# Fetching whole groups of table rows on SyncE: eight rows a step instead of seven, for six groups instead of five

## What is computed

```python
h = relu(layernorm(x))
p1 = tanh(h @ pp_W1 + pp_b1) @ pp_W2 + pp_b2
inter = concat([p1[src], p1[dst]]) @ pi_W1 + pi_b1
inter = (inter @ pi_W2 + pi_b2) @ pi_W3          # (edges, 64 * 8)
i1 = einsum('ecb,eb->ec', inter.reshape(-1, 64, 8), edge_attr)
i1 = tanh(i1 @ ii_W1 + ii_b1) @ ii_W2 + ii_b2
out = x + segment_sum(i1, dst, 6250)
```

## Time and profile before

| | us |
|---|---|
| median of 3 runs | 1965.04 (1964.56 to 1967.29) |
| profiled execution, its own time | 1972.48 |
| its span, first to last instruction | 1970.7 |
| PE busy in the span | 1717.0 (87%) |
| DVE | 1453.4 (74%) |
| ACT | 1109.4 (56%) |
| POOL | 1474.1 (75%) |

### The profile page before, as it was taken

One profiled execution on the slowest core, in us unless ns is written; L12 is line 12 of the kernel. 1 busy time (PEld: TensorE's weight loads), 2 busy tenths in 40 slices (PEclk: granted clock), 3 DMA queues, 4 the chain that ended last, 5 costly groups with the idle time before them and its releaser, 6 DMA issues.

```text
span 1970.7 us, 61801 instructions
## 1 busy us (share of the span) xinstructions
PE 1717.0 (87%) x20012; PEld 1125.7 (57%) x20012; DVE 1453.4 (74%) x1937; ACT 1109.4 (56%) x2419; POOL 1474.1 (75%) x1561
## 2 busy tenths in 40 slices
PE   7699999998888888888888888888888988888998
PEld 6366666665555555555555555555555555555666
DVE  7688778787777777777776777777767767777776
ACT  5666666565555555555555555555555655555554
POOL 7777777777777777777777777777777777777774
PEclk8799999999999999999999999999999999999999
DMA  6543333333333333333323333333333333333332
GB/s 139 123 80 64 67 65 60 65 71 65 58 61 60 58 62 58 66 63 57 62 56 61 62 61 66 62 55 61 57 63 64 60 63 62 57 58 55 57 76 47
DMA packets 271300, 128.56 MB, mean 65 GB/s; under 512 B 192747, under 2 KB 243546, under 8 KB 270959
## 3 DMA queue, kind: packets, MB, share of 16 engines
q0 software_dynamic: 49408, 50.69, 16.5%
q10 hardware_dynamic: 55738, 50.10, 10.6%
q1 hardware_dynamic: 165938, 25.50, 7.9%
HBM read 119.48 MB, written 6.00 MB: 64 GB/s over the span
## 4 chain that ended last, share of the span: by engine, by line
POOL 55%; issue 21%; PE 11%; SPq 9%; DMA 1%; ACT 1%; DVE 0%; ACTq 0%; POOLq 0%; DVEq 0%
POOL u_rows L573 55%; SPq L443 6%; PE bank L1388 4%; SPq L440 2%; PE bank L1371 1%; PE bank L1483 1%; SPq L482 1%; PE bank L1395 1%; PE spread_ps L1380 1%; PE bank L1355 1%; DMA p<-L_gnn_pi_W 0%; DMA v_win<-v_tab 0%; PE spread_ps L1217 0%; DMA u_rows<-u_tab,src_e 0%; PE bank L1223 0%
## 5 line engine op out<-in xcount | busy, mean ns | idle before, releaser
L573 POOL DMA_INDIRECT u_rows<-u_tab,src_e x1416 | 1348.0, 952 | 432.0 <-issue 430.7
L996 DVE TENSOR_TENSOR o_sb<-st_sb,spread_ps 128x2048 f32<-128x2048 f32 x391 | 893.6, 2286 | 403.0 <-PE spread_ps L1380 370.3
L761 ACT ACTIVATE st_sb<-bank,s_bias 64x256 f32<-64x256 f32 x1564 | 734.2, 469 | 452.9 <-PE bank L1371 431.3
L1388 PE MATMUL bank<-o_sb,g_sb 128*64 128x256 f32 x6256 | 792.4, 397 | 1.0 <-DVE o_sb L996 0.8
L1388 PEld LDWEIGHTS bank<-o_sb,g_sb 128*64 128x64 f32 x6256 | 427.3, 140 | 225.2 <-issue 23.9
L1371 PE MATMUL bank<-ident,u_rows 128*128 128x128 f32 x1436 | 257.5, 302 | 196.7 <-DMA u_rows<-u_tab,src_e 195.9
L1060 DVE TENSOR_TENSOR hot_t<-loc_bc,bank 126x512 bf16<-126x512 bf16 x391 | 268.6, 687 | 90.6 <-PE bank L1483 44.8
L1371 PEld LDWEIGHTS bank<-ident,u_rows 128*128 128x128 f32 x1436 | 188.7, 191 | 247.5 <-DMA u_rows<-u_tab,src_e 237.8
L1483 PEld LDWEIGHTS bank<-hot,t_sb 128*65 128x65 f32 x3128 | 215.0, 139 | 148.9 <-issue 146.9
L749 ACT ACTIVATE tt_sb<-bank,z_bias 128x256 f32<-128x256 f32 x391 | 185.5, 474 | 157.1 <-PE bank L1388 157.1
L752 ACT COPY t_sb<-bank 128x256 f32<-128x256 f32 x391 | 146.6, 375 | 213.6 <-PE bank L1395 205.1
(11 more groups left out here) (147 smaller groups left out, 350.7 us busy)
## 6 DMA issues: line engine op xcount, KB each, us to landing
loc_bc<-loc_tab ACTq DMA_DIRECT2D x387, 126.0 KB
sp_stage<-u_tab SPq DMA_DIRECT2D x2560, 0.2 KB
u_rows<-u_tab,src_e POOLq DMA_INDIRECT x1416
v_win<-v_tab SPq DMA_DIRECT2D x391, 15.8 KB
basis<-edge_attr SPq DMA_DIRECT2D x24, 256.0 KB
v_tab<-acc_all SPq DMA_DIRECT2D x6, 336.0 KB
basis<-u_tab,src_e POOLq DMA_INDIRECT x100, 2.9
u_tab<-basis SPq DMA_DIRECT2D x6, 224.0 KB
```

Source lines behind the costliest of these rows:

```text
L573: pool.indirect_dma_start(out=u_rows[:, g % UR, j, :] if g >= AHEAD else first_u[:, g - XG, j, :], out_offset=None, in_=u_tab[:, :], in_of ...
L761: last = nc.scalar.activation(tiles[h * D:(h + 1) * D, j], s_ps[part].rearrange("p (q a e) -> p q a e", q=2, a=TILES), ACT.Identity, bias= ...
L996: return nc.vector.tensor_tensor(o_sb[:, r, :, :].rearrange("p c (j e) -> p j c e", j=TILES), st_sb[:, r, :].rearrange("p (j e) -> p j e", ...
L1388: last = nc.tensor.matmul(z_ps[h * D:(h + 1) * D, 0:2 * P], g_sb[:, c, :], o_sb[:, r, c, 2 * h * P:(2 * h + 2) * P], start=(c == 0), stop= ...
```

## The change

Three constants and the semaphores of the first groups change. SP brings the groups 69, 133, 197, 261, 325 and 389 instead of 83, 157, 231, 305 and 380. It begins each 68 steps before its number, at steps 1, 65, 129, 193, 257 and 321, and needs 64 steps of eight rows. Register loads at L440 take sixteen row numbers instead of eight, so there is one in every other step. The groups 7 to 31 had a semaphore each for POOL's gathers; now two neighbours share one, and TensorE waits for both before it uses the first.

```diff
-    ROWS = 7
-    BY_SP = [(83, 4), (157, 78), (231, 152), (305, 226), (380, 300)]
-    AT_ONCE = 8
+    ROWS = 8
+    BY_SP = [(64 * k + 69, 64 * k + 1) for k in range(6)]
+    AT_ONCE = 16
...
-        first_u_in = sems("first_u_in", AHEAD - XG)
+        first_u_in = sems("first_u_in", (AHEAD - XG + 1) // 2)
...
-                        ).then_inc(u_in[g % UR] if g >= AHEAD else first_u_in[g - XG], 16)
+                        ).then_inc(u_in[g % UR] if g >= AHEAD else first_u_in[(g - XG) // 2], 16)
...
-                        pe.wait_ge(first_u_in[g - XG], 64)
+                        pe.wait_ge(first_u_in[(g - XG) // 2], 64 * min(2, AHEAD - XG - (g - XG) // 2 * 2))
```

## The result

| | before | after |
|---|---|---|
| median, us | 1965.72 (1964.56 to 1967.29, 5 runs) | 1975.99 (1975.16 to 1980.59, 5 runs) |
| profiled execution, its span | 1970.7 | 1978.8 |
| POOL's gathers into `u_rows` | 1416 | 1412 |
| TENSOR_LOAD at L440 | 320, median 783 ns | 192, median 1232 ns |
| POOL held by PE | none beyond the gaps it always has | 14.1 us |

The ratio is 1.0056 with a 95% interval of 1.0044 to 1.0068, so 8.6 to 13.4 us more; the forecast was about 8. Both profiled executions are longer than the medians: that of before took 1972.48 us, 7 more (it isn't among the five), and that of after 1980.59, the longest of its five and 4.6 more. So single times near their ends carry some us of their own.

What follows compares the result with a forecast made beforehand. The prediction took POOL's gathers, 5.03 us a group, to bound the kernel. A 9.8 us hold less 2.2 us gained at the end made +7.6, so 1973 us from a median of 1965.04, range 1964 to 2004.

Steps and rivals of the forecast that it cites:

- What bounds the kernel: POOL's gathers, never held, set the pace from 42.5 us to the end: 1.257 us a gather, 5.03 a group.
- The load of sixteen: SP's register load of sixteen row numbers at L440: taken as 1.20 us, 1.26 with the 0.06 around it.
- SP's step: SP's mean step with eight rows and loads of sixteen: 4.81 us instead of 4.51, between 4.60 and 5.00.
- The start: SP's first windows: window 8 leaves at 98.0, 6.6 us later, and window 33 at 221.5, 13.5 us later.
- The hold: POOL's gathers for group 42 wait for group 34's slot until 230.1: 9.8 us lost, not growing afterwards.
- The end: POOL binds PE to about group 386, which PE can start earlier: 2.2 us gained.
- At nothing: Parts taken to cost nothing: shared semaphores of the first groups, the final move at L451, 512 more row transfers.
- The sum: The whole change: 9.8 - 2.2 = +7.6 us on the profiled execution's 1972.5; predicted 1973 from the median shown, 1965.04.
- A load no dearer than eight's: Rival on SP's register loads: sixteen numbers cost about what eight do, the hold shrinks to 3.1, 1966 us; chance 0.21.
- No hold: Rival at POOL's early slots: PE's early groups don't slip behind them, only the end's gain remains, 1963 us; chance 0.05.
- A dear load: Rival on SP's register loads, up to where SP becomes the bound: 1978 us with 1.33, 2001 with 1.45; chance 0.22.
- SP as the bound throughout: Rival on SP's step: from 4.95 us on, POOL is held again and again; 2024 us at 5.00; chance 0.12.

Runs made afterwards that it cites:

- e3: The kernel before with register loads of sixteen row numbers instead of eight and nothing else; ratio 1.0000 to the kernel before.
- e6: The changed kernel with register loads of eight row numbers instead of sixteen, so one in every step; ratio 1.0213 to the kernel before.
- e5: The changed kernel once more, unchanged, on another chip; ratio 1.0043 to the kernel before, median 1978.04 us.
- e1: The changed kernel with SP's reload of x moved from step 8 to step 200; ratio 1.0051 to the kernel before, median 1979.42 us.
- e4: The changed kernel without group 69, the first of SP's six groups, which POOL gathers itself; ratio 1.0025 to the kernel before.
- e7: The changed kernel with other row counts: 8 in steps 1 to 3, 7 to step 33, then 8, and 9 every tenth; ratio 1.0011 to the kernel before.
- e8: The changed kernel with 23 single tiles on SP instead of whole groups, 7 rows in steps 4 to 59, x reloaded at step 200; ratio 0.9988 to before.
- e11: The single-tile version of e8 once more, on another chip; ratio 0.9975 to the kernel before, 1960.62 against 1966.32 us.
- e2: The kernel before with eight rows a step and loads of sixteen, but its own five groups and first steps; ratio 1.0026 to the kernel before.
- e9: The kernel before with loads of sixteen, plus 44 more single-row transfers on SP in step 20; ratio 1.0030 to the kernel before.
- e10: The kernel before with loads of sixteen, plus 44 more single-row transfers on SP in step 200; ratio 0.9999 to the kernel before.

## Why the prediction was right, point by point

**What bounds the kernel.** Right: POOL's total sets the time, and SP's share of the chain before 440 us is no price by itself (e3).

**The load of sixteen.** 1.232 us (taken: 1.20), so 1.29 with what stands around it. The two readings in the earlier trace rows gave 1.14 and 1.33, and the middle was good. By the 200 ns a register of the Trainium skill (Runtime: NRT & Kernel Launch, Instruction fetch mechanics) eight further ones would have made it 2.4; the trace of after doesn't agree, it has (1.232 - 0.783) / 8 = 0.056 us for each.

**SP's step.** 4.78 us, taken 4.81. With loads of eight it is 4.95, taken 5.0 in e6, so the way in which I added the parts is 0.03 to 0.05 too high a step. For e6, which lies just at POOL's rate, that was half the effect; for the changed kernel it hardly counts. The prediction's tightest later place was right too: group 74, some 2 us to spare; measured 3.7, and 2.6 at group 77.

**The start.** Window 8 left at 99.8 and, in e5, 98.2 (taken: 98.0). Between windows 1 and 2 there are 71.99 - 65.71 = 6.3 us instead of 5.1, and most of that excess is the issue of window 1 itself, 1.10 us instead of 0.32; the rest is 0.45 us before the first load of row numbers, which waits for `sp_idx`. The same code had window 8 at 94.8 in e1, so the 98.0 was within what one execution differs from another by. Window 33: 222.8 and 220.4, taken 221.5.

**The hold.** Right in kind and place, 9.8 taken, 14.1 and 11.7 measured. I moved only groups 33 and 34, but group 32's matmuls too, at 204.45 before, came 14.4 us later, and the first wait is for its slot, at group 40. That moves the place, not the sum. The size was missed by three things: groups 32 to 34 slipped by 14.4 to 14.9 us, not 13.5; POOL came there 2.1 us sooner (its first gather into `u_rows` at 167.6 against 169.7); and groups 44 and 45 added 0.8, where the hold was to end at 42.

**The end.** This is the term that was mis-sized: 2.2 us of gain taken, about 0.2 measured. I let PE use group 386 a median 2.9 after its last gather's start. In the changed kernel that is 1941.73 - 1936.80 = 4.9, as before (5.1); in e5 it is 5.0. What happened stands four groups earlier. SP begins to store a part of the output at 1916.67, the DMA engines are 95% busy from 1917 to 1919, and group 382, whose last gather began at 1916.83, can be used only 5.0 us later. PE, idle for 2.99 us, then has half its clock (0.50, the 1.2 GHz level) from 1921 to 1925; the step takes 6.9 us, and at its own 4.1 to 4.5 a step after that PE isn't back at POOL's pace by 386. The lines are SP's store, group 382 on PE, and two stretches (PE, weight load, DVE, ACT, POOL busy; granted clock; DMA share; GB/s):

```profile
1916.67 0.80 SPq L456 DMA_DIRECT2D out<-x_sb  x2
...
1921.85 1.23 PE L1371 MATMUL bank<-ident,u_rows 128*128 128x128 f32 x4 [2.99 <-DMA u_rows<-u_tab,src_e]
...
1917.00:1919.00 2.00, 1.86 (x26) 1.47 (x22) 1.35 (x2) 0.81 (x3) 1.70 (x2) 1.00 0.95 261
...
1921.00:1925.00 4.00, 3.15 (x28) 2.16 (x30) 1.23 (x1) 1.85 (x4) 3.09 (x4) 0.50 0.20 47
```

The kernel before has the same store, at 1912.86, with the DMA engines 92% busy from 1915 to 1917. There the skip at 380 had put POOL ahead, and PE waited for nothing and kept the full clock. So a place that was free while PE was behind POOL's rows cost time once PE waited for them, like the start. That the store made the gather late is read from the two standing side by side; no run moved the store. In e5 waits of 0.90 and 1.23 us at groups 382 and 383 follow the store, and one of 1.19 at 386. e4 agrees by the time: one skip fewer up to group 388 costs 5.2 us, where a whole group is 5.03.

**At nothing.** The shared semaphores, the last move and the 512 further transfers: PE's waits show no entry for the first groups. The shared semaphores weren't tried alone, but e7, e8 and e11 have them, and e8 and e11 are faster than the kernel before, so they cost nothing that can be seen.

**The sum.** From one profile to the other it closes: the hold is 14.1, POOL's first gather begins 0.8 sooner (41.7 against 42.5), the gathers take 5.1 less, and the end gives 0.2. That makes 8.0, and the spans differ by 8.1; the medians differ by 10.3. The 5.1 wasn't in the prediction: with the gaps and without holds a gather takes 1.2545 us in the changed kernel (1896.8 us for 1512; 1.2543 in e5) and 1.2579 in the kernel before (1906.9 for 1516). It isn't shown to come from the change. Over all profiles it is 1.2548 to 1.2582 with five groups on SP (before, e2, e3, e4, e9, e10) and 1.2543 to 1.2563 with six groups or 23 tiles (after, e1, e5, e6, e7, e8, e11): the ranges overlap, and the profiled execution of before, one of the longest of its kernel, has nearly the longest gathers of all. The prediction added its +7.6 to that execution and then set it on the median. So the forecast of 8 came near the 8.6 to 13.4 partly by luck: the hold was too small by 2 to 4, the end's gain too large by 2, and gathers that differ between executions weren't seen.

**The rivals.** A load no dearer than eight's: fell, 1.232. No hold: fell. A dear load, or SP as the bound throughout: fell, but only by 0.17 us a step (4.78 against 4.95): in e6 the same kernel at 4.95 loses another 33 us. e1, whose hold was shorter and whose median wasn't, speaks against none of this: in its profiled execution the hold is 5.3 less than in the changed kernel's, the first gather 0.7 sooner and the gathers 2.7 longer in all, 3.3 less together, and the span is 4.0 shorter. What stays open is what makes the start of SP and POOL's gathers differ from one execution to the next.

## What to carry to other kernels

Before an engine that feeds the bound one is given more work, look for the place where the bound engine has the least room (here 3.7 us of free slots at group 42, against 33 us later on) and ask what will be late there; work on SP that was free at step 200 cost time at step 20, all of it that the room didn't take. The share of the chain that lies on an engine isn't what it costs: SP went from 9 to 54% in a version that is faster. Look at the link by which the chain reaches that engine, and whether the bound engine was held there at all. And work is better taken off the bound engine in pieces so small that the last of them still comes in time to be used; here 23 tiles up to group 380 gave what six groups up to 389 didn't, though that version differs in more than this.

## What the runs showed that I had not expected

A register load on SP takes 0.47 us for one number (once), 0.78 for eight and 1.23 for sixteen, so it pays to load many at once. Single-row transfers issued in a row with 16 numbers used again and again took 15.27 / 44 = 0.35 us each, not the 0.41 of those with new numbers; only 9 of the 44 have the register arithmetic of an address before them, where each of the others has it. And the pitch of POOL's gathers differs by up to 4 ns from one profile to the next (1.2543 to 1.2582 us), which with 1500 of them is 6 us, as much as the effects that were to be measured here. So small effects should be read from holds and gaps in the traces, and from medians of several executions, not from the span of one profile.
